# The last MLP of a two-layer graph kernel in three split passes, and the identity and two bias additions on GpSimd

## The chip, the cores and the metric

The kernel runs on one core of one Trainium2 chip. The metric is the device time of one execution in microseconds (us). Three executions of the kernel before gave 590.76, 591.12 and 591.52 us; the median is 591.12. In the profiled execution the granted TensorE clock was 0.998 of full speed (2.4 GHz).

## The reference, cut to what matters

`adj` is a 4096 x 4096 matrix A, `x` and `x2` are 4096 x 128. All is float32.

```
ax1 = A @ x ; ax2 = A @ x2
h1  = (2 + eps1) * ax1 ; h2 = (2 + eps2) * ax2
for i in range(3):                          # the MLP, for each of the two branches
    h1 = relu(h1 @ W1[i].T + b1[i]) ; h2 = relu(h2 @ W2[i].T + b2[i])
x   = layernorm(x + concat(h1, h2) @ Wm.T + bm)
Ah  = A + I ; d = rsqrt(rowsum(Ah))
out = layernorm(x + (d[:, None] * Ah * d[None, :]) @ x @ W.T + b)
```

## The kernel before, in words

**Split numbers.** A float32 matrix product is made from three passes of a faster format, fp32r: each operand is a rounded part `hi` and a rest `lo = value - hi`, and the passes are hi\*hi, hi\*lo and lo\*hi. For every tile of A (128 rows of 1024 columns, `raw`), ScalarE (ACT) rounds it to `ahi` (L723), VectorE (DVE) makes the rest `alo` (L920) and TensorE (PE) multiplies it (L536). `x1hi` and `x1lo` are the other operand, split the same way.

**Tiles and stages.** A layer is four quarters of 32 tiles. In layer 0 a tile takes 12 matmuls of 512 columns, for `x` and `x2`, and DVE also adds every tile to the row sums (L931, L935). In layer 1 it takes 6. Layer 1 is `ps <- (A + I) @ y`, where y is the normalised output of layer 0 times d. I stands on the diagonal, so it is added to one square of 128 x 128 in 32 of the 128 tiles, in place in `raw` (L1095 and L1102), before ACT rounds them. The tiles of layer 1 are called L1.0, L1.1 and so on here, in the order in which PE takes them. The first 24 are of quarter 0, then 8 of quarter 1, then the last 8 of quarter 0 (`woven`).

**Who runs ahead.** ACT rounds up to 4 tiles ahead of PE in layer 0 and 6 in layer 1 (the wait on `block_used` before L723), DVE follows ACT. Each engine runs a fixed list in program order; nothing is reordered when it runs.

**The MLP.** The MLP of a quarter runs in the quarter behind it, its steps slotted between tiles by tables: `PE_DENSE` (behind which tile PE runs each of the three dense layers), `PE_MERGE` (the product with Wm), `ACT_RELU`, `DVE_SPLIT_H`. The second entry of each pair, plan 1, is for the MLP of the last quarter, which runs beside the first tiles of layer 1. A dense step is four pieces `m` of 128 x 512. In plan 1 the first dense layer, behind tile L1.1, is plain float32 with `par` and `h` as they are; it waits for `h_ready` alone. The other two are split, in three passes with `hhi` (from ACT, L749) and `h_rest` (from DVE, L942).

**What hangs on the last MLP.** Merge, residual, statistics, the power of -0.5 on GpSimd (POOL, L1246), then `yt` and its rounding on ACT and `x1lo` on DVE (L1074), behind tile L1.25. PE needs them at L1.32. ACT then also writes the last quarter of `xn` (L756). The second residual bases (`xn <- xn + b`, L1079, 128 x 1024 each) are made on DVE, the third behind L1.58 and the fourth behind L1.92.

**GpSimd before.** It makes constants at the start and then only powers of 128 x 8 and smaller (L1241, L1246).

Of the kernel before, what the change touches and what calls it, by code (L numbers as in the profile page):

```python
# [37 lines left out]
M = 2 * CH  # L38
# [30 lines left out]
PE_DENSE = ({3: 0, 5: 1, 8: 2}, {1: 0, 3: 1, 5: 2})  # L69
PE_MERGE = (10, 6)  # L70
DVE_SPLIT_H = {4: 1, 6: 2}
# [6 lines left out]
ACT_RELU = ({k + SPLIT: l for k, l in PE_DENSE[0].items()}, {4: 0, 6: 1, 7: 2})  # L78
# [7 lines left out]
ACT_NORM_LAST = 29  # L86
# [4 lines left out]
ACT_NORM = (22, 20)  # L91
ACT_COPY_AY = 3
DVE_MAKE_Y = (KB + 4, 2 * KB + 4, 3 * KB + 3, 23)
# [3 lines left out]
DVE_SECOND_BASE = DVE_SPLIT_Y[:2] + (JB + 26, 2 * JB + 28)  # L97
AHEAD = 3
AHEAD2 = 5
# [23 lines left out]
def build(nc, a_t, head, early, x12, params, scratch, out):  # L123
    with ExitStack() as ctx:  # L124
# [368 lines left out]
        def _(pe):  # L493
# [48 lines left out]
            def dense(q, l, plan):  # L542

                for m in range(M):

                    if plan == 0:
                        wait(pe, hlo_ready, q * (LAYERS * M) + (M * l + m + 1))
                        passes = ((whi, hhi), (whi, hlo), (wlo, hhi))
                    elif l:
                        wait(pe, hlo_ready, q * (LAYERS * M) + (M * (l - 1) + m + 1))  # L550
                        passes = ((whi, hhi), (whi, h_rest), (wlo, hhi))
                    else:
                        wait(pe, h_ready, q * (4 * M) + (M * l + m + 1))
# [127 lines left out]
        def _(act):  # L681
# [214 lines left out]
        def _(dve):  # L896
# [40 lines left out]
            def split_h(q, l, m, plan):  # L937
# [3 lines left out]
                wait(dve, hhi_ready, q * (LAYERS * M) + (M * (l - plan) + m + 1))  # L941
# [148 lines left out]
            def add_identity(q, n):  # L1090

                wait_raw1(dve, q, n)
                k = n % KB
                square = raw_tile(1, n)[:, k * P:(k + 1) * P]
                dve.tensor_tensor(square, square, identity[:, :], ALU.add).then_inc(identity_added, 1)  # L1095

            def add_identities_last(n):

                wait_unit(dve, n)
                for at in squares_of(n):  # L1100
                    square = raw_tile(1, n)[:, at:at + P]
                    dve.tensor_tensor(square, square, identity[:, :], ALU.add).then_inc(identity_added, 1)  # L1102

# [28 lines left out]
            def layer0_quarter(q, before):  # L1132
                for n in range(JB):
# [8 lines left out]
                    if q is QUARTERS - 1:  # L1142
# [5 lines left out]
                        if n >= JB - KB:  # L1148
                            add_identity(0, n + KB - JB)

            def layer1_first():

                for p in range(2 * JB):
                    split_a(p // JB, 1, p % JB)
                    if p < JB:
                        mlp_step(LAST, p, 1)
                        y_step(p, (LAST,))
                        if p in DVE_SPLIT_H:
                            for m in range(M):
                                split_h(LAST, DVE_SPLIT_H[p], m, 1)  # L1160
                    finish_step(0, p - FIRST_ENDS - 1)
                    if p == DVE_SECOND_BASE[2]:
                        second_base(2)
                    if JB <= p and (p - JB + AHEAD2) // KB == 1:
                        add_identity(1, p - JB + AHEAD2)

            def layer1_quarter(q, before):
                for n in range(JB):
# [4 lines left out]
                    if q * JB + n == DVE_SECOND_BASE[3]:  # L1173
                        second_base(3)
                    if q == LAST:
                        for i in range(0 if n == 0 else n + AHEAD2, min(n + AHEAD2 + 1, JB)):
                            if squares_of(i):
                                add_identities_last(i)
                    elif (n + AHEAD2) // KB == q:
                        add_identity(q, n + AHEAD2)  # L1180
# [56 lines left out]
        def _(pool):  # L1237
# [4 lines left out]

            def norm_power(done, r=slice(0, KB)):
# [21 lines left out]
            for q in range(QUARTERS - 1):  # L1265
                norm_power(q + QUARTERS + 1)
# [45 lines left out]
```

## Time and profile before

| What | Value |
|---|---|
| median of 3 runs | 591.12 us |
| the profiled execution's own time | 591.38 us |
| its span, first to last instruction | 589.6 us |
| PE busy | 583.0 us, 99% |
| DVE busy | 545.4 us, 93% |
| ACT busy | 378.8 us, 64% |
| POOL busy | 28.1 us, 5% |

The span is the stretch from the first to the last instruction on the chip; the time holds 1.8 us more around it. Busy time of PE counts matmuls whose ends are modelled, so two starts in a row say more than a duration. On DVE and ACT a row's duration overlaps the next instruction a little: two DVE operations of 1024 columns last 1.21 us each and start 1.14 us apart. Where the text says pitch, it means from start to start.

### The profile page before, as it was taken

To read this page: it belongs to the slowest core of one execution; us is meant where nothing else is said; L and a number is where in the kernel's file an instruction comes from. 1 tells how busy PE (TensorE), PEld (TensorE's weight loads), DVE (VectorE), ACT (ScalarE), POOL (GpSimd) and SP (SyncE) were. 2 spreads that over 40 slices of the span, in tenths; PEclk is the share of its full clock that TensorE was granted. 3 is DMA by queue.
4 is the path that set the end of the run, shared out by engine and by line. 5 is a ranking of instruction groups with operands and counts; after the bars stand their busy time and mean duration, and the time that the engine had idled before them with its cause. 6 is when DMAs were issued, how large, how long until landed. Compare 5 with 4: busy or idle time off the path is not lost.

```text
span 589.6 us, 7659 instructions
## 1 busy us (share of the span) xinstructions
PE 583.0 (99%) x2676; PEld 485.9 (82%) x2676; DVE 545.4 (93%) x695; ACT 378.8 (64%) x512; POOL 28.1 (5%) x26
## 2 busy tenths in 40 slices
PE   9999999999999999999999999999999999999996
PEld 8888888888888888888888888878888888888885
DVE  6999999998988998898799999997999997989986
ACT  6544437852454773453667336479799799799794
POOL 0000000001100000110000020000200001010011
PEclk9999999999999999999999999999999999999999
DMA  8968565443655544354544374776899999999921
GB/s 330 397 248 294 206 223 206 145 148 143 207 196 179 179 169 145 142 197 178 195 147 143 143 268 187 261 287 222 316 365 392 425 377 340 387 338 367 387 77 72
DMA packets 31131, 141.91 MB, mean 241 GB/s; under 512 B 5504, under 2 KB 6272, under 8 KB 17024
## 3 DMA queue, kind: packets, MB, share of 16 engines
q1 hardware_dynamic: 30528, 139.87, 64.6%
q10 hardware_dynamic: 576, 1.70, 0.7%
q8 instruction: 14, 0.23, 0.2%
q14 instruction: 13, 0.11, 0.1%
HBM read 139.40 MB, written 2.16 MB: 240 GB/s over the span
## 4 chain that ended last, share of the span: by engine, by line
PE 97%; ACT 1%; DVE 1%; issue 1%; POOLq 0%; POOL 0%; DVEq 0%
PE ps L536 81%; PE pd L557 6%; PE ps L612 6%; PE pd L566 2%; PE pd L598 1%; PE pd L664 1%; ACT outn L756 0%; ACT ahi L723 0%; DVE z L1217 0%; ACT ahi_extra L723 0%; DVE stats L1222 0%; POOLq L124 0%; POOL rstd L1246 0%; DVE mv L1007 0%; DVE vareps L1014 0%
## 5 line engine op out<-in xcount | busy, mean ns | idle before, releaser
L723 ACT ACTIVATE ahi<-raw 128x1024 fp32r<-128x1024 f32 x212 | 222.6, 1060 | 162.5 <-PE ps L536 156.3
L920 DVE TENSOR_TENSOR alo<-raw,ahi 128x1024 fp32r<-128x1024 f32 x212 | 256.5, 1218 | 27.0 <-ACT ahi L723 26.0
L536 PE MATMUL ps<-ahi,x2s 128*128 128x512 f32 x512 | 138.4, 389 | 0.0
L536 PE MATMUL ps<-ahi,x1hi 128*128 128x512 f32 x384 | 121.9, 393 | 0.0
L536 PE MATMUL ps<-ahi,x1lo 128*128 128x512 f32 x384 | 120.9, 390 | 0.0
L536 PE MATMUL ps<-alo,x1hi 128*128 128x512 f32 x384 | 120.6, 390 | 0.0
L536 PEld LDWEIGHTS ps<-ahi,x2s 128*128 128x128 f32 x512 | 96.4, 188 | 20.1
L536 PEld LDWEIGHTS ps<-alo,x1hi 128*128 128x128 f32 x384 | 72.2, 188 | 15.1
L536 PEld LDWEIGHTS ps<-ahi,x1lo 128*128 128x128 f32 x384 | 72.3, 188 | 15.0
L536 PEld LDWEIGHTS ps<-ahi,x1hi 128*128 128x128 f32 x384 | 71.9, 188 | 15.0 <-issue 0.7
L536 PE MATMUL ps<-alo,x2s 128*128 128x512 f32 x256 | 80.2, 389 | 0.0
L931 DVE TENSOR_TENSOR rowsum<-rowsum,raw 128x1024 f32<-128x1024 f32 x60 | 73.0, 1216 | 0.0
L935 DVE TENSOR_TENSOR rowsum<-rowsum,raw 128x1024 f32<-128x1024 f32 x56 | 68.1, 1216 | 0.0
L536 PEld LDWEIGHTS ps<-alo,x2s 128*128 128x128 f32 x256 | 48.0, 188 | 10.0
L920 DVE TENSOR_TENSOR alo_extra<-raw,ahi_extra 128x1024 fp32r<-128x1024 f32 x42 | 50.8, 1221 | 3.9 <-ACT ahi_extra L723 3.6
L723 ACT ACTIVATE ahi_extra<-raw 128x1024 fp32r<-128x1024 f32 x42 | 43.8, 1060 | 2.7 <-PE ps L536 1.8
L744 ACT ACTIVATE h<-pd,par 128x512 f32<-128x512 f32 x48 | 31.8, 695 | 1.0 <-PE pd L557 1.0
L1246 POOL TENSOR_TENSOR rstd<-vareps,halves 128x8 f32<-128x8 f32 (+2 forms) x10 | 20.3, 2025 | 184.0 <-DVE vareps L1125 138.4
L1241 POOL TENSOR_TENSOR degpow<-degc,halves 128x8 f32<-128x8 f32 x4 | 6.6, 1640 | 373.6 <-DVE degpos L985 373.6
L942 DVE TENSOR_TENSOR hlo<-h,hhi 128x512 fp32r<-128x512 f32 x36 | 22.6, 683 | 0.0
L728 ACT ACTIVATE hhi<-h 128x512 fp32r<-128x512 f32 x36 | 22.0, 629 | 0.8
L536 PE MATMUL ps<-alo_extra,x1hi 128*128 128x512 f32 x64 | 20.0, 389 | 0.0
(103 smaller groups left out, 526.6 us busy)
## 6 DMA issues: line engine op xcount, KB each, us to landing
raw<-a_t SPq DMA_DIRECT2D x108, 1024.0 KB, 4.9
raw<-a_t SPq DMA_DIRECT2D x32, 512.0 KB, 7.4
raw<-early SPq DMA_DIRECT2D x7, 512.0 KB, 7.5
xn<-x SPq DMA_DIRECT2D x2, 1024.0 KB, 7.8
xn<-x SPq DMA_DIRECT2D x3, 512.0 KB, 10.5
out<-outn ACTq DMA_DIRECT2D x3, 512.0 KB, 6.6
par<-params SPq DMA_DIRECT2D x1, 708.0 KB, 12.4
raw<-head SPq DMA_DIRECT2D x2, 256.0 KB, 3.1
```

The lines of the kernel that those rows point to most:

```text
L536: mm = pe.matmul(ps[bank + (CH * (q % 2) if layer else 0)][:, :], block_of(w, n), a[c], start=(n == 0 and k == 0), stop=(n == JB - 1 and k ...
L557: mm = pe.matmul(pd[:, m, :], w[:, at:at + P], a[:, m, :], start=(k == 0), stop=(k == len(passes) - 1))
L566: mm = pe.matmul(merged[:, k, :], h[:, CH * b + k // 4, (k % 4) * P:(k % 4 + 1) * P], par[:, WM_AT + b * P:WM_AT + (b + 1) * P], start=(k ...
L612: mm = pe.matmul(bank, block_of(w, j + t), a[:, at], start=(n == opens and t == 0 and k == 0), stop=(n == closes and t == 1 and k == 2), s ...
L723: act.activation(ring_hi(layer, q, n), raw_tile(layer, n), ACT.Copy).then_inc(hi_ready, 1)
L728: act.activation(hhi[:, m, :], h[:, m, :], ACT.Copy).then_inc(hhi_ready, 1)
L744: act.activation(h[:, m, :], pd[:, m, :], ACT.Relu, bias=par[:, at:at + 1]).then_inc(h_ready, 1)
L920: dve.tensor_tensor(ring_lo(layer, q, n), raw_tile(layer, n), as_f32(ring_hi(layer, q, n)), ALU.subtract).then_inc(lo_ready, 1)
L931: dve.tensor_tensor(rowsum[:, :], rowsum[:, :], tile, ALU.add).then_inc(rowsum_step, 1)
L935: dve.tensor_tensor(to[:, :], rowsum[:, :], tile, ALU.add).then_inc(raw_used, 1)
L942: dve.tensor_tensor((hlo, h_rest)[plan][:, m, :], h[:, m, :], as_f32(hhi[:, m, :]), ALU.subtract).then_inc(hlo_ready, 1)
L1246: pool.tensor_tensor(rstd[:, r], vareps[:, r], halves[:, r], ALU.pow).then_inc(rstd_ready, 1)
```

## The change: what it does

1. The first dense layer of the last MLP becomes split, as the other two are: ACT rounds `h` to `hhi` (four pieces, behind its tiles 3 and 4), DVE makes `h_rest`, PE runs 12 passes in place of 4 plain float32 products. All three dense layers and the merge go behind later tiles: 4, 6, 8 and 10 in place of 1, 3, 5 and 6.
2. DVE makes `h_rest` in two parts, two pieces behind one tile and two behind the next, three times. Before it was four pieces behind one tile, twice.
3. The steps behind the merge go with it: `yt`, its rounding and `x1lo` come 4 tiles later (L1.29 for `x1lo`), and the last quarter of `xn` comes 3 tiles later.
4. The 32 additions of the identity and the second bases of quarters 2 and 3 go from DVE to GpSimd, in its program order: 8 identities, the powers of the last quarter, 8 identities, both bases, then powers and identities in turn.

```diff
-PE_DENSE = ({3: 0, 5: 1, 8: 2}, {1: 0, 3: 1, 5: 2})
-PE_MERGE = (10, 6)
-DVE_SPLIT_H = {4: 1, 6: 2}
+PE_DENSE = ({3: 0, 5: 1, 8: 2}, {4: 0, 6: 1, 8: 2})
+PE_MERGE = (10, 10)
+DVE_SPLIT_H = {3: (0, 0), 4: (0, 2), 5: (1, 0), 6: (1, 2), 8: (2, 0), 9: (2, 2)}
...
-ACT_RELU = ({k + SPLIT: l for k, l in PE_DENSE[0].items()}, {4: 0, 6: 1, 7: 2})
+ACT_RELU = ({k + SPLIT: l for k, l in PE_DENSE[0].items()}, {7: 0, 9: 1, 10: 2})
...
-ACT_NORM_LAST = 29
+ACT_NORM_LAST = 32
...
-ACT_NORM = (22, 20)
+ACT_NORM = (22, 24)
...
-DVE_MAKE_Y = (KB + 4, 2 * KB + 4, 3 * KB + 3, 23)
+DVE_MAKE_Y = (KB + 4, 2 * KB + 4, 3 * KB + 3, 27)
...
-                    elif l:
-                        wait(pe, hlo_ready, q * (LAYERS * M) + (M * (l - 1) + m + 1))
+                    else:
+                        wait(pe, hlo_ready, q * (LAYERS * M) + (M * l + m + 1))
                         passes = ((whi, hhi), (whi, h_rest), (wlo, hhi))
-                    else:
-                        wait(pe, h_ready, q * (4 * M) + (M * l + m + 1))
-                        passes = ((par, h),)
...
-                if plan == 0 and n in (ACT_EVACUATE[0] + 1, ACT_EVACUATE[0] + 2):
+                if n in (ACT_EVACUATE[plan] + 1, ACT_EVACUATE[plan] + 2):
                     for m in range(CH):
-                        round_h(q, 0, CH * (n - ACT_EVACUATE[0] - 1) + m)
+                        round_h(q, 0, CH * (n - ACT_EVACUATE[plan] - 1) + m)
...
-                        if n >= JB - KB:
-                            add_identity(0, n + KB - JB)
...
-                            for m in range(M):
-                                split_h(LAST, DVE_SPLIT_H[p], m, 1)
+                            l, first = DVE_SPLIT_H[p]
+                            for m in range(first, first + CH):
+                                split_h(LAST, l, m, 1)
...
+            for n in range(KB):
+                add_identity(0, n)
             degree_power(QUARTERS - 1)
             norm_power(QUARTERS)
...
+            for n in range(KB, 2 * KB):
+                add_identity(1, n)
+            pool.wait_ge(xn_ready, 2 * QUARTERS)
+            pool.wait_ge(yt_ready, LAST)
+            for q in range(2, QUARTERS):
+                pool.tensor_tensor(quarter(xn, q), quarter(xn, q), bias_rows(BO_AT), ALU.add).then_inc(base_ready, 1)
```

On DVE at the seam of the layers, the kernel before ran this. The first row is the identity of L1.7, the `x3` are the rests of L1.0 to L1.2, and the `alo` behind the reduction is that of L1.3:

```order
L1095 TENSOR_TENSOR raw<-raw,identity 128x128
L920 TENSOR_TENSOR alo<-raw,ahi 128x1024 x3
L964 STREAM_TRANSPOSE outn<-rowsum_all 128x1024
L970 TENSOR_REDUCE partial<-outn 128x32
L920 TENSOR_TENSOR alo<-raw,ahi 128x1024
L920 TENSOR_TENSOR alo_extra<-raw,ahi_extra 128x1024
L942 TENSOR_TENSOR h_rest<-h,hhi 128x512 x4
L920 TENSOR_TENSOR alo_extra<-raw,ahi_extra 128x1024
L920 TENSOR_TENSOR alo<-raw,ahi 128x1024
L942 TENSOR_TENSOR h_rest<-h,hhi 128x512 x4
```

The changed kernel runs this in the same place (its lines L915, L959, L965 and L937 are L920, L964, L970 and L942 of the kernel before):

```order
L915 TENSOR_TENSOR alo<-raw,ahi 128x1024 x3
L959 STREAM_TRANSPOSE outn<-rowsum_all 128x1024
L965 TENSOR_REDUCE partial<-outn 128x32
L915 TENSOR_TENSOR alo<-raw,ahi 128x1024
L937 TENSOR_TENSOR h_rest<-h,hhi 128x512 x2
L915 TENSOR_TENSOR alo_extra<-raw,ahi_extra 128x1024
L937 TENSOR_TENSOR h_rest<-h,hhi 128x512 x2
L915 TENSOR_TENSOR alo_extra<-raw,ahi_extra 128x1024
L937 TENSOR_TENSOR h_rest<-h,hhi 128x512 x2
L915 TENSOR_TENSOR alo<-raw,ahi 128x1024
L937 TENSOR_TENSOR h_rest<-h,hhi 128x512 x2
```

The identities are gone from DVE, and each of the rests of L1.4, L1.5, L1.6 and L1.7 now stands behind two pieces of `h_rest`.

On PE, the plain float32 layer stood behind the two first tiles of layer 1 (here the end of L1.0, then L1.1, the layer, and L1.2):

```order
L536 MATMUL ps<-alo,x1hi 128x512
L536 MATMUL ps<-ahi,x1hi 128x512 x2
L536 MATMUL ps<-ahi,x1lo 128x512 x2
L536 MATMUL ps<-alo,x1hi 128x512 x2
L557 MATMUL pd<-h,par 128x512 x4
L536 MATMUL ps<-ahi,x1hi 128x512 x2
L536 MATMUL ps<-ahi,x1lo 128x512 x2
L536 MATMUL ps<-alo,x1hi 128x512 x2
```

Now PE goes from tile L1.2 through L1.3 and L1.4 before it reaches the first piece of the split layer:

```order
L534 MATMUL ps<-ahi,x1hi 128x512 x2
L534 MATMUL ps<-ahi,x1lo 128x512 x2
L534 MATMUL ps<-alo,x1hi 128x512 x2
L534 MATMUL ps<-ahi,x1hi 128x512 x2
L534 MATMUL ps<-ahi,x1lo 128x512 x2
L534 MATMUL ps<-alo,x1hi 128x512 x2
L534 MATMUL ps<-ahi_extra,x1hi 128x512 x2
L534 MATMUL ps<-ahi_extra,x1lo 128x512 x2
L534 MATMUL ps<-alo_extra,x1hi 128x512 x2
L552 MATMUL pd<-hhi,whi 128x512
L552 MATMUL pd<-h_rest,whi 128x512
L552 MATMUL pd<-hhi,wlo 128x512
```

PE takes five tiles of A in a row there, where before it took two.

## Rows read from the trace of the kernel before

**Rows 1.** Part 1 of the page: engine, busy us, share of the span, instructions.
```profile
PE 583.0 (99%) x2676; PEld 485.9 (82%) x2676; DVE 545.4 (93%) x695; ACT 378.8 (64%) x512; POOL 28.1 (5%) x26
```

**Rows 2.** Waits of PE, whole span: us in total, times, longest.
```profile
PE pd L664 <- DVE blank L1182: 1.1, 1, 1.1
PE pd L598 <- DVE h L1211: 0.5, 1, 0.5
```

**Rows 3.** Timeline of PE at the seam of the layers: start us, us, what.
```profile
386.98 0.39 PE L536 MATMUL ps<-alo,x1hi 128*128 128x512 f32 x1
...
390.61 0.61 PE L536 MATMUL ps<-ahi,x1hi 128*128 128x512 f32 x2
...
391.51 0.62 PE L536 MATMUL ps<-alo,x1hi 128*128 128x512 f32 x2
391.97 3.59 PE L557 MATMUL pd<-h,par 128*128 128x512 f32 x8
...
396.77 0.62 PE L536 MATMUL ps<-ahi,x1hi 128*128 128x512 f32 x2
...
398.13 0.39 PE L557 MATMUL pd<-hhi,whi 128*128 128x512 f32 x1
...
400.85 0.62 PE L536 MATMUL ps<-ahi_extra,x1hi 128*128 128x512 f32 x2
```

**Rows 4.** Timeline of DVE before and at the seam, no idle time between.
```profile
368.16 0.27 DVE L1095 TENSOR_TENSOR raw<-raw,identity 128x128 f32<-128x128 f32 x1
368.36 1.21 DVE L920 TENSOR_TENSOR alo<-raw,ahi 128x1024 fp32r<-128x1024 f32 x1
...
385.47 1.21 DVE L920 TENSOR_TENSOR alo<-raw,ahi 128x1024 fp32r<-128x1024 f32 x1
...
387.95 3.48 DVE L920 TENSOR_TENSOR alo<-raw,ahi 128x1024 fp32r<-128x1024 f32 x3
391.35 1.23 DVE L964 STREAM_TRANSPOSE outn<-rowsum_all 128x1024 f32<-128x1024 f32 x1
...
393.75 1.22 DVE L920 TENSOR_TENSOR alo<-raw,ahi 128x1024 fp32r<-128x1024 f32 x1
...
396.01 2.54 DVE L942 TENSOR_TENSOR h_rest<-h,hhi 128x512 fp32r<-128x512 f32 x4
```

**Rows 5.** Timeline of ACT in its activations of the MLP.
```profile
393.61 0.68 ACT L749 ACTIVATE hhi<-pd,par 128x512 fp32r<-128x512 f32 x1
394.18 0.69 ACT L744 ACTIVATE h<-pd,par 128x512 f32<-128x512 f32 x1
```

**Rows 6.** Timeline of POOL: a one-input pass of 128 columns, then powers.
```profile
1.18 0.29 POOL L1250 TENSOR_SCALAR_AFFINE_SELECT identity<-identity 128x128 f32<-128x128 f32 x1 [0.24 <-POOL identity L1248]
...
240.83 1.64 POOL L1241 TENSOR_TENSOR degpow<-degc,halves 128x8 f32<-128x8 f32 x1 [84.62 <-DVE degpos L985]
252.43 2.57 POOL L1246 TENSOR_TENSOR rstd<-vareps,halves 128x8 f32<-128x8 f32 x1 [9.96 <-DVE vareps L1014]
```

**Rows 7.** Timeline of DVE around the second of those powers.
```profile
252.28 1.23 DVE L920 TENSOR_TENSOR alo<-raw,ahi 128x1024 fp32r<-128x1024 f32 x1
253.42 1.23 DVE L931 TENSOR_TENSOR rowsum<-rowsum,raw 128x1024 f32<-128x1024 f32 x1
254.57 1.21 DVE L920 TENSOR_TENSOR alo<-raw,ahi 128x1024 fp32r<-128x1024 f32 x1
255.70 1.21 DVE L935 TENSOR_TENSOR rowsum<-rowsum,raw 128x1024 f32<-128x1024 f32 x1
```

**Rows 8.** Timeline of DVE beside the first of those powers.
```profile
240.86 0.28 DVE L999 BATCH_NORM_STATS2 stats<-z 128x6 f32<-128x128 f32 x1
```

**Rows 9.** Timeline of DVE behind `x1lo`: rests of L1.26 and L1.27.
```profile
436.54 2.35 DVE L920 TENSOR_TENSOR alo<-raw,ahi 128x1024 fp32r<-128x1024 f32 x2
```

**Rows 10.** Timeline of PE: its first use of the rest of L1.26.
```profile
438.07 0.62 PE L536 MATMUL ps<-alo,x1hi 128*128 128x512 f32 x2
```

**Rows 11.** Timeline of ACT: the last block of `xn` of the last quarter.
```profile
447.25 0.49 ACT L756 ACTIVATE xn<-z,nshift,rstd 128x128 f32<-128x128 f32 x1
```

More of the change, by code:

```diff
@@ L96 @@
 DVE_SPLIT_Y = tuple(k + 2 for k in DVE_MAKE_Y)
-DVE_SECOND_BASE = DVE_SPLIT_Y[:2] + (JB + 26, 2 * JB + 28)
-AHEAD = 3
-AHEAD2 = 5
+DVE_SECOND_BASE = DVE_SPLIT_Y[:2]
 DVE_RESIDUAL2 = PE_PROJECT + SPLIT2
@@ L940, in split_h @@
                     wait(dve, h_ready, q * (4 * M) + (M * l + m + 1))
-                wait(dve, hhi_ready, q * (LAYERS * M) + (M * (l - plan) + m + 1))
+                wait(dve, hhi_ready, q * (LAYERS * M) + (M * l + m + 1))
                 dve.tensor_tensor((hlo, h_rest)[plan][:, m, :], h[:, m, :], as_f32(hhi[:, m, :]),
@@ L1088, in y_step @@
                         second_base(g)
[L1090 to L1102, printed above, removed]
             def residual2(q, k):
@@ L1158, in layer1_first @@
                         if p in DVE_SPLIT_H:
-                            for m in range(M):
-                                split_h(LAST, DVE_SPLIT_H[p], m, 1)
+                            l, first = DVE_SPLIT_H[p]
+                            for m in range(first, first + CH):
+                                split_h(LAST, l, m, 1)
                     finish_step(0, p - FIRST_ENDS - 1)
[L1162 to L1165, printed above, removed]
             def layer1_quarter(q, before):
@@ L1172, in layer1_quarter @@
                     finish_step(before, n)
[L1173 to L1180, printed above, removed]
             dve.memset(blank[:, :], 0.0).then_inc(blank_ready, 1)
@@ L1241, in degree_power, with add_identity, add_identities_last @@
                 pool.tensor_tensor(degpow[:, :], degc[:, :], halves[:, :], ALU.pow).then_inc(degpow_ready, 1)
+            def add_identity(q, n):
+                wait_raw1(pool, q, n)
+                k = n % KB
+                square = raw_tile(1, n)[:, k * P:(k + 1) * P]
+                pool.tensor_tensor(square, square, identity[:, :], ALU.add).then_inc(identity_added, 1)
+            def add_identities_last(n):
+                wait_unit(pool, n)
+                for at in squares_of(n):
+                    square = raw_tile(1, n)[:, at:at + P]
+                    pool.tensor_tensor(square, square, identity[:, :], ALU.add).then_inc(identity_added, 1)
             def norm_power(done, r=slice(0, KB)):
@@ L1262, in _ @@
                 norm_power(q + 1)
+            for n in range(KB):
+                add_identity(0, n)
             degree_power(QUARTERS - 1)
             norm_power(QUARTERS)
-            for q in range(QUARTERS - 1):
-                norm_power(q + QUARTERS + 1)
+            for n in range(KB, 2 * KB):
[4 more added lines that the diff above has]
+                pool.tensor_tensor(quarter(xn, q), quarter(xn, q), bias_rows(BO_AT), ALU.add).then_inc(base_ready, 1)
+            for q in range(2, QUARTERS):
+                if q == LAST:
+                    for n in range(JB):
+                        if squares_of(n):
+                            add_identities_last(n)
+                    norm_power(2 * QUARTERS - 1)
+                else:
+                    norm_power(QUARTERS + 1)
+                    for n in range(q * KB, q * KB + KB):
+                        add_identity(q, n)
+                    norm_power(QUARTERS + q)
             for g, (k0, k1) in enumerate(TAIL):
```

## The prediction

> **What bounds the kernel now.** I read part 1 of the page first: PE is busy 99% of the span, DVE 93% [rows 1]. Then the waits of PE: 1.1 us at the start and 0.5 us near the end, and none between [rows 2]. So the time is PE's own work, and only two things move it: less work on PE, or a wait that PE does not have now. The third view was the timeline of PE and DVE at the seam of the layers, to see how far DVE is ahead. The rest of the last tile of layer 0 is done at 385.47 + 1.21 = 386.68, and PE uses it at 386.98, 0.30 us later [rows 3, 4]. DVE runs without a gap there. So DVE is almost the bound at the seam.
>
> **PE's own work.** A tile of layer 1 takes 391.97 - 390.61 = 1.36 us. The plain float32 layer: it starts at 391.97, and L1.3 starts at 396.77, with L1.2 between, so it takes 396.77 - 1.36 - 391.97 = 3.44 us. A split layer takes 400.85 - 398.13 = 2.72 us [rows 3]. The gain is 3.44 - 2.72 = 0.72 us. The merge and all else of PE stay.
>
> **What DVE sheds.** An identity costs DVE 368.36 - 368.16 = 0.20 us of pitch [rows 4]. 8 of them stand ahead of L1.0 (7 ahead of the tile with 0.30 us left), 8 more beside L1.35 to L1.42, 16 later, where DVE has 2 us or more in hand for most tiles and PE waits for nothing: those are worth nothing. The second bases are shed late as well.
>
> **What it costs when POOL reads SBUF.** No row has a sum of this size on POOL. But the powers tell something. The same power of 128 x 8 lasts 1.64 us where POOL starts it beside a `BATCH_NORM_STATS2` of DVE, which has one input [rows 8], and 2.57 us where it starts 0.15 us into a rest of 1024 columns [rows 6, 7]. The surplus, 0.93 us, is what was left of that operation (253.42 - 252.43 = 0.99). So POOL waits for a DVE operation with two SBUF inputs. In the other direction the next DVE operation starts on time, at 253.42, inside the power, but it takes 254.57 - 253.42 = 1.15 us of pitch where its neighbour takes 1.13: some 0.01 to 0.015 us for the 8 columns that POOL reads. So the two share a read path, and DVE pays about the time that POOL reads. For 128 columns this is 16 times as much, 0.16 to 0.24 us; for 1024 columns 1.3 to 1.9. The bounds are 0 (no hold) and the 0.29 us of the one-input pass of 128 columns [rows 6], 8 times that or 2.3 us for a base. I take the value nearest to DVE's own pitch for the same columns, 0.2 us, and 1.6 for a base.
>
> The page SBUF — State Buffer of the Trainium skill (section Who interferes with whom) says that a VectorE instruction with two SBUF inputs contends with a GpSimd instruction that reads SBUF, and that whoever issues first has the pair for its whole instruction. By that rule, the trace agrees in one direction (POOL waited 0.93 us) and not in the other: DVE started at 253.42 inside a power that ran to 255.00. The GPSIMD Engine Reference (section 3.1) gives 4497 ns for a `tensor_tensor` add of 2048 float32 columns, so an estimate from that page is 2.25 us for one base and 0.28 for an identity.
>
> **Dense stage, step by step.** With 0.2 us an identity the 8 POOL additions (all done before L1.0: DVE finds the tiles landed for its own from 368.16 on [rows 4]) cost DVE what the 8 it sheds gave back. The rest of L1.0 starts at 387.95 as before, and the `alo` of L1.3 at 393.75, ready at 394.95 [rows 4]. PE has no dense layer ahead of it now: L1.3 starts at 390.61 + 2 x 1.36 = 393.33 and needs the rest 391.51 - 390.61 = 0.90 us later, at 394.23 [rows 3]. Wait: 0.7 to 0.8. Then DVE has 2 `h_rest` (2.54 / 4, or 0.62 of pitch each [rows 4]) ahead of the rest of L1.4: 394.89 + 1.24 + 1.21 = 397.34, while PE wants it at 394.23 + 0.75 + 1.36 = 396.34. Wait: 1.0. The dense layer then ends at 400.6. `relu` on ACT can start at 398.7, gives one `h` and one `hhi` every 1.14 us (2 x 0.57 [rows 5]), so the second `hhi` is there at 401.3. The rest of L1.6 is queued behind its `h_rest` on DVE: 401.3 + 0.62 + 1.21 = 403.1, and PE wants it at 400.6 + 1.36 + 0.90 = 402.85. Wait: 0.3. From L1.7 on PE's two dense layers give DVE 5.4 us and I find no further wait. Sum: 2.1 us. If POOL cost DVE nothing, DVE would be 1.6 us earlier, the first two waits would shrink to 0.2, and the sum would be 0.5 us: the last wait hangs on ACT and stays.
>
> **Behind the merge.** `x1lo` is 4 tiles later, and so is the low point of DVE's lead behind it: before, the rest of L1.26 is ready at 436.54 + 1.21 = 437.75 and used at 438.07, 0.3 us left [rows 9, 10]; now this is L1.30. From there DVE gains 1.36 - 1.14 = 0.22 us a tile, while the 8 identities that POOL adds there, as their tiles land, take 0.2 each. When POOL gets to the bases, DVE has about 0.5 us in hand and not the 2 it has before. They start when the last block of `xn` is done, which is at 447.25 + 0.49 now [rows 11] and 3 tiles and 2 us later after the change, near 454. Two bases of 1.6 us hold DVE 3.2 us, with one or two rests between; 3.2 - 0.5 - 2 x 0.2 = 2.3 us of wait, and 0.1 us at L1.30. The 1.7 us of the projection behind L1.41 come too late to help. Later identities on POOL cost DVE what it sheds.
>
> **Sum.** -0.72 + 2.1 + 0.1 + 2.3 = +3.8 us. The profiled execution took 591.38 us (span 589.6), which makes 595.2; it lies 0.26 us over the median of 591.12, so on the scale of the median I forecast 594.9 us. What a measurement of this kernel can tell from no change is 0.2%, 1.2 us.
>
> **The rivals.**
>
> *No hold: DVE really is relieved.* Then POOL's sums are free, DVE is 1.6 us earlier at the seam and PE waits 0.5 us in the dense stage: -0.72 + 0.5 = -0.2 us, 590.9. For it: DVE starts on time inside a power. Against it: the 0.93 us that POOL loses, and the 0.01 us of DVE behind the power. It decides where an identity costs DVE under 0.07 us, for then the two first waits of the dense stage stay under 0.5 us and the gain of PE covers them. It cannot be faster by more than 0.72 us, 0.12%, since no other work of PE goes. This is the side on which the forecast of slower is wrong.
>
> *Identities hold DVE, the bases do not.* A long sum on POOL could be read in pieces between DVE's operations, or come when DVE has more in hand than my 0.5 us. Then the last term falls away: -0.72 + 2.1 = +1.4, or 592.5. For it: POOL always gave way to an operation under way. Against it: even in pieces the columns are the same.
>
> *POOL holds for its whole operation.* With 0.29 us an identity and 2.3 a base: the last tile of layer 0 waits 8 x 0.29 - 7 x 0.20 - 0.30 = 0.6 us, the dense stage 2.2, behind L1.30 it loses 0.3 and some 0.06 a tile, and the bases 2 x 2.3 - 0.7: together 0.6 + 2.2 + 0.6 + 3.9 - 0.7 = +6.6, 597.7. It is the rule of the page above with a price from a row; DVE's start at 253.42 speaks against it.
>
> **How the numbers follow.** I give the forecast 0.45, the bases without a hold 0.18, no hold at all 0.25, the hold of the whole operation 0.12. Range: from the rival without a hold (590.8) to just below the whole hold (597.4). Slower by over 0.2%: 0.45 + 0.12 + most of 0.18 makes 0.72. Within 0.2%: 0.25, which is the rival without a hold and a part of the second. Faster by over 0.2% needs more than PE has to give: 0.03.
>
> **What would show it.** In the profile after: the first dense layer as 12 passes in 2.72 us; waits of PE on `alo` at L1.3, L1.4 and L1.6 of 0.7, 1.0 and 0.3 us and again of 1 us and more near 456 and 458 us, beside the two bases on POOL; POOL's identities lasting 1 us and more where they start inside a DVE operation, and DVE operations of 1.4 us instead of 1.2 beside them. If the rests of DVE keep a pitch of 1.14 us beside POOL's sums, the hold is wrong, and with it 1.6 us of the dense stage and all of the last term. If waits of PE stand at the bases and not at the seam, the chain of the dense stage is wrong.

## The result and the profile after

The changed kernel takes 599.16 us (median of 4 executions, 598.23 to 600.42) against 591.32 us of the kernel before, measured beside it (4 executions). The ratio is 1.0131 with a 95% interval of 1.0117 to 1.0145: it is slower by 7.8 us. The forecast was slower by 3.8 us, to 594.9, and its range ended at 597.4. The sign held; the size did not.

The profiled execution took 598.23 us with a span of 596.4; before it was 591.38 and 589.6. Part 1 of the page after answers to [rows 1]:

```profile
PE 585.3 (98%) x2680; PEld 486.6 (82%) x2680; DVE 548.9 (92%) x665; ACT 381.0 (64%) x516; POOL 82.6 (14%) x60
```

DVE has 30 instructions less and is busy 3.5 us more. The waits of PE, of which before only those for `blank` and `h` stood there [rows 2]:

```profile
PE ps L534 <- DVE alo L915: 3.8, 2, 2.1
PE pd L659 <- DVE blank L1150: 1.1, 1, 1.1
PE ps L534 <- DVE alo_extra L915: 0.7, 1, 0.7
PE pd L593 <- DVE h L1179: 0.5, 1, 0.5
```

The view lists no wait below some tenths, so the timeline of PE is read by starts. A pair of matmuls takes 0.45 us from start to start. At the seam of the layers, in place of [rows 3]:

```profile
393.63 0.61 PE L534 MATMUL ps<-ahi,x1lo 128*128 128x512 f32 x2
394.32 0.73 PE L534 MATMUL ps<-alo,x1hi 128*128 128x512 f32 x2
...
395.35 0.62 PE L534 MATMUL ps<-ahi_extra,x1lo 128*128 128x512 f32 x2
396.66 0.72 PE L534 MATMUL ps<-alo_extra,x1hi 128*128 128x512 f32 x2 [0.69 <-DVE alo_extra L915]
397.22 0.40 PE L552 MATMUL pd<-hhi,whi 128*128 128x512 f32 x1
...
399.98 0.61 PE L534 MATMUL ps<-ahi_extra,x1hi 128*128 128x512 f32 x2
...
401.79 0.61 PE L534 MATMUL ps<-ahi,x1lo 128*128 128x512 f32 x2
402.52 0.72 PE L534 MATMUL ps<-alo,x1hi 128*128 128x512 f32 x2
```

The rest of L1.3 comes 394.32 - 393.63 - 0.45 = 0.24 us late, that of L1.4 0.86 and that of L1.6 0.28; each time the matmuls behind the wait start another 0.11 late. The split layer takes 399.98 - 397.22 = 2.76 us. The second place is beside the two bases on POOL:

```profile
455.22 0.63 PE L534 MATMUL ps<-ahi,x1lo 128*128 128x512 f32 x2
457.53 0.74 PE L534 MATMUL ps<-alo,x1hi 128*128 128x512 f32 x2 [1.69 <-DVE alo L915]
...
458.35 0.40 PE L534 MATMUL ps<-ahi,x1lo 128*128 128x512 f32 x1
460.84 0.79 PE L534 MATMUL ps<-alo,x1hi 128*128 128x512 f32 x1 [2.10 <-DVE alo L915]
461.43 0.63 PE L534 MATMUL ps<-ahi,x1hi 128*128 128x512 f32 x1
461.86 0.63 PE L534 MATMUL ps<-ahi,x1lo 128*128 128x512 f32 x1
...
463.56 0.86 PE L534 MATMUL ps<-ahi_extra,x1lo 128*128 128x512 f32 x2
```

PE waits 1.86 + 0.11 and 2.27 + 0.36 us. Then six matmuls start 0.43 us apart in place of 0.227. The table by stretches of the same kernel gives the granted clock. Behind the length of the stretch stand the busy us of PE, of its weight loads, of DVE, ACT and POOL, each with its instructions; the last three columns are the granted clock of PE, the DMA share and GB/s:

```profile
456.00:460.00 4.00, 1.21 (x4) 0.67 (x4) 4.00 (x2) 0.86 (x1) 3.70 (x2) 1.00 0.59 242
460.00:462.00 2.00, 1.16 (x3) 0.97 (x4) 2.00 (x3) 0.33 (x1) 0.00 (x0) 0.66 0.21 25
462.00:465.00 3.00, 3.00 (x11) 2.34 (x10) 3.00 (x3) 2.32 (x4) 0.00 (x0) 0.66 0.90 333
```

PE was busy 1.21 of the 4 us between 456 and 460; behind that its clock was at the lower level, 1.2 GHz, for a part of two stretches, then back at 2.4. That costs 6 x 0.20 us, and 0.25 of the 0.36 above.

What POOL does, in place of [rows 6], and the VectorE operations beside it:

```profile
353.49 2.53 POOL L1216 TENSOR_TENSOR raw<-raw,identity 128x128 f32<-128x128 f32 x2
...
376.19 14.85 POOL L1216 TENSOR_TENSOR raw<-raw,identity 128x128 f32<-128x128 f32 x1 [17.21 <-DMA raw<-a_t]
...
453.15 6.55 POOL L1254 TENSOR_TENSOR xn<-xn,par 128x1024 f32<-128x1024 f32 x2
```

```profile
354.22 1.48 DVE L1064 TENSOR_TENSOR yt<-xn,dall 128x1024 f32<-128x1024 f32 x1
355.62 1.48 DVE L915 TENSOR_TENSOR alo<-raw,ahi 128x1024 fp32r<-128x1024 f32 x1
...
387.24 3.48 DVE L915 TENSOR_TENSOR alo<-raw,ahi 128x1024 fp32r<-128x1024 f32 x3
390.64 1.23 DVE L959 STREAM_TRANSPOSE outn<-rowsum_all 128x1024 f32<-128x1024 f32 x1
...
454.06 6.72 DVE L915 TENSOR_TENSOR alo<-raw,ahi 128x1024 fp32r<-128x1024 f32 x2
```

An operation of DVE beside an identity lasts 1.48 us and not 1.21: an identity holds DVE 0.27 us. The two rests beside the bases take 460.71 - 454.06 = 6.65 us from start to start (the next row of that view starts at 460.71); without a hold it would be 2 x 1.135 = 2.27. So a base holds DVE 2.19 us. And one identity took 14.85 us: it started at 376.19 and ended at 391.04, in the transpose.

### The profile page after: what moved, and what is told of

It is laid out like the page before. It is cut to its first block, busy times and chain, and to the rows that moved or that the text cites. A ratio compares the mean times of both kernels' runs of the same rounds, so it can differ in the third digit from the quotient of the medians.

```text
span 596.4 us, 7680 instructions
## 1 busy us (share of the span) xinstructions
PE 585.3 (98%) x2680; PEld 486.6 (82%) x2680; DVE 548.9 (92%) x665; ACT 381.0 (64%) x516; POOL 82.6 (14%) x60
## 4 chain that ended last, share of the span: by engine, by line
PE 81%; DVE 9%; ACT 6%; issue 2%; POOL 1%; POOLq 0%; DVEq 0%; ACTq 0%
PE ps L534 72%; DVE alo L915 5%; PE pd L552 4%; DVE alo_extra L915 2%; PE pd L561 2%; ACT ahi L718 2%; ACT h L739 1%; POOL rstd L1228 1%; PE pd L593 1%; ACT hhi L744 1%; ACT ahi_extra L718 1%; PE ps L607 1%; PE pd L659 1%; ACT outn L808 1%; ACT yt L781 0%
## 5 line engine op out<-in xcount | busy, mean ns | idle before, releaser
L915 DVE TENSOR_TENSOR alo<-raw,ahi 128x1024 fp32r<-128x1024 f32 x212 | 263.0, 1249 | 25.6 <-ACT ahi L718 23.7
L915 DVE TENSOR_TENSOR alo_extra<-raw,ahi_extra 128x1024 fp32r<-128x1024 f32 x42 | 51.6, 1239 | 7.8 <-ACT ahi_extra L718 7.1
L1216 POOL TENSOR_TENSOR raw<-raw,identity 128x128 f32<-128x128 f32 x24 | 37.8, 1597 | 42.8 <-DMA raw<-a_t 42.8
L723 ACT ACTIVATE hhi<-h 128x512 fp32r<-128x512 f32 x40 | 24.4, 630 | 0.8
L937 DVE TENSOR_TENSOR hlo<-h,hhi 128x512 fp32r<-128x512 f32 x36 | 22.6, 681 | 0.0
```

The source lines that it names most:

```text
L723: act.activation(hhi[:, m, :], h[:, m, :], ACT.Copy).then_inc(hhi_ready, 1)
L915: dve.tensor_tensor(ring_lo(layer, q, n), raw_tile(layer, n), as_f32(ring_hi(layer, q, n)), ALU.subtract).then_inc(lo_ready, 1)
L937: dve.tensor_tensor((hlo, h_rest)[plan][:, m, :], h[:, m, :], as_f32(hhi[:, m, :]), ALU.subtract).then_inc(hlo_ready, 1)
L1216: pool.tensor_tensor(square, square, identity[:, :], ALU.add).then_inc(identity_added, 1)
```

## The experiments

The kernel before was run beside each group: 591.71 us for the first four (14 executions), 591.50 for the next four (19), 591.79 for the d group and c2 (13), 591.51 for c3 and c4 (21). Intervals are of the ratio to it. "Theory 1" is that of the prediction with the sizes read from the trace after.

| Kernel | us | ratio, 95% | against before |
|---|---|---|---|
| a1 the split last MLP alone | 593.77 | 1.0036, 1.0022 to 1.0050 | +2.1 |
| a2 the POOL additions alone | 595.37 | 1.0073, 1.0051 to 1.0095 | +3.7 |
| a3 changed, bases on DVE | 593.21 | 1.0025, 1.0015 to 1.0034 | +1.5 |
| a4 changed, identities on DVE | 598.10 | 1.0108, 1.0091 to 1.0125 | +6.4 |
| a5 = a1 with 8 narrow identities | 593.17 | 1.0023, 1.0013 to 1.0034 | +1.7 |
| b1 changed, bases 40 us later | 595.47 | 1.0064, 1.0048 to 1.0079 | +4.0 |
| b2 changed, bases in 16 pieces | 595.84 | 1.0073, 1.0058 to 1.0089 | +4.3 |
| c1 = a1 in another order | 592.26 | 1.0009, 1.0000 to 1.0018 | +0.8 |
| c2 = c1, fourth base behind L1.108 | 593.62 | 1.0028, 1.0018 to 1.0038 | +1.8 |
| c3 = c1, both bases into gaps of DVE | 591.75 | 1.0007, 0.9998 to 1.0017 | +0.2 |
| c4 = before, bases moved as in c3 | 591.72 | 1.0001, 0.9992 to 1.0010 | +0.2 |
| d0 changed kernel again, one execution | 597.56 | | |
| d1 changed, one base on POOL | 595.69 | 1.0070, 1.0056 to 1.0084 | +3.9 |
| d2 changed, 8 small operations more | 601.07 | 1.0168, 1.0147 to 1.0190 | +9.3 |

### The two parts apart

a1 has parts 1 to 3 of the change and leaves the additions on DVE; a2 has part 4 alone.

> Only the MLP part of the change; the identities and all four second bases stay on VectorE. Theory 1 (what GpSimd reads holds VectorE back, and the MLP's new order costs only the waits of the dense stage): PE gains 0.72 us and waits 0.8 + 1.0 + 0.3 = 2.1 us at L1.3, L1.4 and L1.6, so +1.4 us against the kernel before (some 592.7), and no wait of PE near 456 us, no stretch at half clock. Rival (the MLP's new order is the cause, GpSimd innocent): +5 us or more, with the two long waits near 456 us still there.

> Only the GpSimd part of the change; the MLP as in the kernel before. Theory 1: no wait at the seam (four identities at 0.27 us take less from VectorE than eight at 0.20 gave back), but the two bases on GpSimd hold VectorE 2.2 us each with some 1.3 us in hand, so PE waits about 3 us near 455 us, and perhaps 1 us more at half clock: +3 to +4 us (594.5). Rival (the MLP is the cause): within 1 us of the kernel before.

The waits of PE in a1, then in a2 (without the two that every kernel has):

```profile
PE ps L536 <- DVE alo_extra L917: 0.7, 1, 0.7
PE ps L536 <- DVE alo L917: 0.6, 1, 0.6
...
PE ps L609 <- DVE alo L917: 0.3, 1, 0.3
```

```profile
PE ps L536 <- DVE alo_extra L920: 3.0, 3, 1.7
```

So each part is slower by itself, and by its own waits: the first at the seam, the second beside the bases. a2 has nothing at the seam. Its two waits beside the bases come to 3.03 us by starts; the third of the view stands far behind them, at 538.8 us, and costs 0.79. By starts the seam of a1 costs 2.24 us, which with the 0.7 gained makes 1.5; the other 0.6 us of its 2.1 are taken up with c1. Neither shows a lower clock there. 2.1 + 3.7 = 5.8, and the change costs 7.8; by the spans of the profiled executions it is 2.2 + 3.9 = 6.1 against 6.8. In the change the bases find DVE without a lead and the clock falls; against that, its profile lacks the waits near 536 to 539 us that a1 and a2 have, and its seam costs 0.5 us less than that of a1.

### Which addition costs

```diff
+                    if q * JB + n == DVE_SECOND_BASE[3]:      # a3: bases back on DVE (third likewise)
+                        second_base(3)
```

> The whole change, but the last two second bases back on VectorE where they were. Theory 1: the waits of 1.9 and 2.3 us and the 1.2 us at half clock near 456 to 464 us go, the dense stage keeps its 1.7 us: +1.0 to +1.5 us against the kernel before (592.5). Rival (identities on GpSimd are the heavier part): +4 us or more.

> The whole change, but the 32 identities back on VectorE; the last two second bases on GpSimd. Theory 1: dense stage 2.1 us, bases 4.4 us of hold with 1.0 us in hand and 0.4 us gained between, so 3 us of wait, then 0 to 1.2 us at half clock: +4.5 to +5.5 us (596.3). Rival (identities are the heavier part): under +2 us.

With the identities alone on POOL (a3) the time is that of a1 within the intervals. The profile of a3 has 0.5 us less of wait at the seam (0.35 us in place of 0.90 at L1.3), and that is what moving the identities off DVE gave there. a4 cost 6.4 us, a little over theory 1, but by another path. Its first base did not hold DVE where it was issued; it was shut out itself. POOL in a4:

```profile
454.22 17.41 POOL L1262 TENSOR_TENSOR xn<-xn,par 128x1024 f32<-128x1024 f32 x2 [22.12 <-ACT xn L753]
```

The first of the two lasted 14.07 us and got in only when DVE came to its first `z <- pd` operation, at 465.95. That operation was not held; the rest behind it was, for 1.94 us, and likewise with the second base. So both holds fell on the chain from `z` to the normalised output, and PE waited for its end at the projection:

```profile
498.16 2.05 PE L595 MATMUL pd<-par,h 128*128 128x128 f32 x16 [2.19 <-ACT h L802]
```

### Is the price the reading time, and is it paid anywhere

b1 has POOL add the bases behind its next power, near 493 us. b2 adds them at the old place in 16 pieces of 128 columns.

```diff
+                for k in range(KB):                           # b2
+                    i = pool.tensor_tensor(quarter(xn, q)[:, k:k + 1, :], quarter(xn, q)[:, k:k + 1, :], ...)
```

> The whole change, with the two bases on GpSimd moved behind the power of the first quarter of layer 1 (near 494 us), where VectorE is 5 us or more ahead. Theory 1 (a base on GpSimd holds VectorE some 2.2 us, and it costs time only where VectorE is not ahead): VectorE's operations beside the bases still take 3.4 us, but PE does not wait for them and stays at full clock; the time is that of the kernel with the bases on VectorE, +1.5 us against the kernel before (593.2). Rival (the place matters little; GpSimd's two long additions cost some 5 us wherever they stand): +6 us or more.

> The whole change, with each of the two bases on GpSimd written as 8 additions of 128 columns. Theory 1 (the hold is GpSimd's reading time, 0.27 us for 128 columns, taken once for each of its instructions): the same 4.3 us of hold, but one piece beside each VectorE operation, so VectorE makes up 0.22 us a tile in between: no wait over 0.6 us, no half clock, +2.0 to +3.0 us against the kernel before. Rival (the hold is mostly a fixed price of each GpSimd instruction, over 0.3 us): 16 instructions cost 8 us or more of hold and the time is no better than the change's own, +7 us.

The bases of b2, then the first of b1, then what DVE did beside that one:

```profile
454.04 22.32 POOL L1271 TENSOR_TENSOR xn<-xn,par 128x128 f32<-128x128 f32 x16
```

```profile
492.98 2.39 POOL L1271 TENSOR_TENSOR xn<-xn,par 128x1024 f32<-128x1024 f32 x1
```

```profile
493.05 2.35 DVE L1127 TENSOR_TENSOR nshift<-nmean,rstd 128x8 f32<-128x8 f32 x1 [0.40 <-POOL rstd L1244]
```

An operation of 8 columns, which takes 0.17 us in the kernel before, took 2.35: the hold, 2.2 us, does not depend on what DVE does. In b2 the 16 pieces follow each other every 1.40 us. Ten of them hold a rest of DVE 0.27 us each. From 468.93 us on DVE alternates between `z <- pd` and rests; the last six pieces get in beside the `z` and hold nothing. The last two held rests and the first free one:

```profile
466.13 2.88 DVE L917 TENSOR_TENSOR alo_extra<-raw,ahi_extra 128x1024 fp32r<-128x1024 f32 x2
...
469.20 1.22 DVE L917 TENSOR_TENSOR alo<-raw,ahi 128x1024 fp32r<-128x1024 f32 x1
```

So the hold in b2 is 10 x 0.27 = 2.7 us in all and not the 4.3 that theory 1 had. A fixed price of each GpSimd instruction is refuted even so: 8 pieces of 0.27 make the 2.19 of one base. In pieces or later, the long waits and the lower clock go (the largest wait beside the bases of b2 is 0.37 us), and the time falls from 599.2 to 595.8 and 595.5. Theory 1 had said +2 to +3 for b2 and +1.5 for b1. It missed what comes later: PE waits 1.1 us at the projection for `h` from ACT, and 0.4 to 0.5 near 539 us for `ahi`. By the order of the instructions the pause of DVE is handed on through the chain `nmean`, squares, `vareps`, power, `nshift`, output; no run cuts this chain.

### The seam

a5 is a1 with the first 8 identities added in one column of 128 only, so part of the identity is left out. That takes about 1 us off DVE ahead of L1.0.

```diff
+                width = 1 if q == 0 else P
+                dve.tensor_tensor(square[:, 0:width], square[:, 0:width], identity[:, 0:width], ALU.add)
```

> Only the MLP part, all additions on VectorE, and the first eight identities are added in one column of their squares instead of 128 (this leaves out part of the computation): VectorE is relieved of about 0.13 us each, 1.0 us before L1.0. Theory 1 (the waits at L1.3 and L1.4 hang on how far VectorE is behind at the seam, the one at L1.6 on ScalarE): PE waits 1.1 us instead of 2.1 in the dense stage, +0.4 us against the kernel before, 1 us under the kernel with the MLP part alone. Rival (the waits hang on the order alone): no less than that kernel, +2 us.

The waits at the seam fell by 1.0 us, from 2.24 to 1.23, so DVE's lateness is what PE waits for there. The time fell by 0.4 only; in this profile 0.5 us of wait also stands near 112 us, in layer 0, where nothing was edited. c1 takes nothing off DVE and changes its order: the rests of L1.3, L1.4 and L1.6 come ahead of the `h_rest`, the reduction of the row sums moves from behind L1.2 to behind L1.5, and the last dense layer comes one tile later.

```diff
+PE_DENSE = ({3: 0, 5: 1, 8: 2}, {4: 0, 6: 1, 9: 2})
+DVE_SPLIT_H = {4: 0, 6: 1, 9: 2}
+DVE_REDUCE_LAST = 5
+ACT_RELU = (..., {7: 0, 9: 1, 11: 2})
```

> The MLP part with everything on VectorE, and VectorE's order changed: the reduction of the transposed row sums (1.14 us) moves from behind L1.2 to behind L1.5, the four h_rest of the first dense layer stand behind the rest of L1.4 and those of the second behind L1.6, those of the third behind L1.9; the third dense layer runs behind L1.9 and its relu behind ScalarE's tile 11. Theory 1 (the dense stage loses only because h_rest and the reduction stand ahead of the rests of L1.3, L1.4 and L1.6): PE waits 0.2 us in all, and 0.5 us of the 0.72 us of PE's gain is left: -0.5 us against the kernel before (0.999). Rival (VectorE is short of time there, whatever the order): waits of 1 us or more come back elsewhere and it is +0.5 us or slower.

No matmul between 385 and 417 us is late in c1. From the first matmul behind the merge of the third quarter to the first behind the projection of layer 1's first quarter, the kernel before takes 460.63 - 332.03 = 128.60 us and c1 461.62 - 333.63 = 127.99. So PE's gain of 0.6 us is there. To the first matmul behind a later projection it is 564.41 - 332.03 = 232.38 and 566.19 - 333.63 = 232.56: all of it is lost again. (This profile is of the slowest of 11 executions and has 1.4 us of wait in layer 0, so only differences inside layer 1 are taken from it.) The waits of PE in c1 that the kernel before does not have (the first is in layer 0):

```profile
PE pd L555 <- DVE hlo L940: 0.6, 1, 0.6
...
PE ps L610 <- DVE alo L918: 0.3, 1, 0.3
PE ps L537 <- DVE alo L918: 0.2, 1, 0.2
```

### Where the gain of the shorter layer goes

The last two stand near 536 and 539 us, just behind the fourth base, and a1, a3 and a5 have one or both. Three kernels asked why. c2 moves that base far back; c3 moves both bases to where DVE waits for ACT anyway; c4 is c3's control.

```diff
-DVE_SECOND_BASE = DVE_SPLIT_Y[:2] + (JB + 26, 2 * JB + 28)
+DVE_SECOND_BASE = DVE_SPLIT_Y[:2] + (JB + 26, 3 * JB + 12)      # c2
+DVE_SECOND_BASE = DVE_SPLIT_Y[:2] + (2 * JB + 3, 2 * JB + 27)   # c3, c4
```

> The reordered split layer (all additions on VectorE) with the fourth second base behind tile L1.108 in place of L1.92. In the reordered kernel PE waited 0.38 us near 536 and 0.32 us near 539, just behind that base and four identities, where VectorE is the later engine by 1 us against the kernel before, since it has four pieces of h_rest (2.5 us) more. Theory 1 (those waits are what is left of its +0.5 us): they go, nothing comes in their place, and the time is 0.7 us under the reordered kernel's: 0.2 us under the kernel before, 591.3 if that has 591.5, ratio 0.9997. Theory 2 (the rest of the +0.5 us is in the start of the kernel and has nothing to do with the edit): no wait at 536 to 542, and the ratio stays 1.0009.

> The reordered split layer with both last second bases moved, all additions on VectorE: the third from behind L1.58 to behind L1.67, the fourth from behind L1.92 to behind L1.91. Both new places are just ahead of a stretch in which VectorE waits for ScalarE anyway (1.73 us at 494.4 us and 0.82 us at 529.9 in the reordered kernel). Theory 1 (what the reordered kernel loses is that VectorE, with 2.5 us of h_rest more, is 1 us later against TensorE, so that the chain nmean, squares, vareps, nshift, normalisation, ahi is late at 536 to 540 us): the chain is 1.1 us earlier, PE waits nowhere between 385 and 565 us, and the time is 0.6 to 0.7 us under the reordered kernel's 592.3 and under the kernel before by 0.3: 591.4 where that has 591.7, ratio 0.9995. Theory 2 (the place of the bases has nothing to do with it, as the base moved to L1.108 seemed to say): the waits of 0.36 and 0.29 us near 535 and 538 stay, ratio 1.001 to 1.002.

> The kernel before with the same two bases moved to the same places and nothing else. Theory 1: PE waits nowhere in that stretch already, so nothing is won: ratio 1.000 within 0.001. Theory 2 (moving the bases is worth something or costs something by itself): ratio outside of 0.999 to 1.001.

In c2 the waits stayed, now mostly for `ahi` from ACT, and a new one of 0.8 us came at a projection, at 565.5 us, for `h` from ACT. Both of its theories fell: the waits stayed, and moving the base cost. c3 is where the kernel before is, within the interval, and no better: theory 2 was right on the waits, and the ratio lies between the two. c4 is as forecast. Its waits:

```profile
PE ps L610 <- DVE alo L918: 0.3, 1, 0.3
PE ps L537 <- ACT ahi L698: 0.2, 1, 0.2
```

They are still there. The reason is in DVE's first rest behind the normalisation of the first output quarter, in c3 and then in c4:

```profile
492.68 1.23 DVE L918 TENSOR_TENSOR alo<-raw,ahi 128x1024 fp32r<-128x1024 f32 x1 [0.59 <-ACT ahi L721]
```

```profile
492.78 1.23 DVE L920 TENSOR_TENSOR alo<-raw,ahi 128x1024 fp32r<-128x1024 f32 x1 [0.59 <-ACT ahi L723]
```

The base was absorbed in both (the idle time before this rest is 0.59 us and not the 1.73 of c1), but the rest itself starts at the same time, though PE is 1.05 us earlier in c3 (first projection of the next quarter at 494.37 against 495.42). What sets it starts at `nmean`, at 474.66 us in c3 and 474.42 in the kernel before, and the bases stand behind that. I read this as DVE and ACT setting the pace of the chain from about 440 to 540 us; this is argued from the timelines, and no run tests it by itself. In the kernel before, DVE has 0.4 us in hand there, at its least. PE's 0.7 us come on top, DVE is 0.2 to 0.4 us later for its four `h_rest` more, and PE waits for the difference. So the shorter layer on PE is worth nothing that shows in any of these orders. That this would turn if DVE had less to do between 440 and 474 us was not tried.

### The clock and the shut-out

> The changed kernel once more, for one profile. In its first profile TensorE's granted clock was 0.66 in the two stretches 460 to 462 and 462 to 465 us, and six matmuls there started 0.43 us apart in place of 0.227, which cost 1.2 us. Theory 1: the fall of the clock belongs to this order of waits (1.86 and 2.27 us, 3 us apart, beside the two bases on GpSimd) and comes again; span 596.4 us within 0.3. Theory 2: it was a chance of that one execution; the waits are the same, the clock stays near 1, and the span is 595.2 us.

> The changed kernel with only the third second base on GpSimd; the fourth goes back to VectorE behind tile L1.92, where the kernel before has it. Theory 1 (each base on GpSimd holds VectorE 2.2 us, and two long waits in a row bring the clock down): the wait near 455 us stays at 1.9 us, the one near 458 (2.3 us) goes, the six slow matmuls (1.2 us) go, and up to 0.3 us comes back behind L1.92; 599.2 - 2.4 - 1.2 + 0.3 = 595.9 us. Theory 2 (the clock falls after any wait of near 2 us): the slow stretch stays, 597.1 us. Theory 3 (the cost is in the late chain, not in the hold): under 1 us is won, 598.2 or more.

> The changed kernel with one small VectorE operation more behind each of the last 8 tiles of layer 0 (a copy of 128 x 8, one SBUF input, near 0.08 us). In the changed kernel one identity on GpSimd began at 376.19 us and ended at 391.04, just after VectorE's first operation with one input (the transpose at 390.64). Theory 1 (between back-to-back VectorE operations with two SBUF inputs GpSimd does not get in, and any operation with one input lets it in): no identity on GpSimd lasts over 2.7 us, all 8 are made before 389 us and hold VectorE 0.27 us each, so the rest of L1.0 comes 4 x 0.27 + 8 x 0.08 = 1.7 us later and the waits of the dense stage grow by about as much: 600.5 to 601 us. Theory 2 (the small operation lets nothing in, or what let GpSimd in at 391 was something else): one identity again lasts over 10 us, only the 0.6 us of the small operations are added: 599.8 us.

d0 is the changed kernel unchanged. In this execution the transfers let POOL come to the bases at 455.7 us and not 453.15. The same table by stretches, of d0 and then of d1 and d2:

```profile
456.00:460.00 4.00, 2.95 (x13) 1.87 (x11) 4.00 (x2) 3.77 (x6) 4.00 (x2) 1.00 0.98 340
462.00:465.00 3.00, 1.49 (x11) 1.40 (x12) 3.00 (x3) 0.75 (x2) 0.38 (x1) 1.00 0.53 131
```

```profile
456.00:460.00 4.00, 2.31 (x10) 1.43 (x9) 4.00 (x3) 1.66 (x3) 0.82 (x1) 1.00 0.71 277
```

```profile
460.00:462.00 2.00, 0.06 (x1) 0.06 (x1) 2.00 (x2) 0.00 (x0) 0.80 (x1) 0.88 0.00 0
462.00:465.00 3.00, 3.00 (x7) 2.40 (x8) 3.00 (x3) 1.55 (x3) 0.00 (x0) 0.51 0.59 180
```

In d0 PE waits 1.39 and 1.84 us (0.11 more behind each), the clock stays at 1.00 and the time is 597.56 us. It has another wait that the first profile has not, 0.75 us at 541.0 for `alo_extra`. In d1 the wait of 1.86 us stands alone, the clock stays at 1.00 and the time is 595.69, as theory 1 had it (595.9): the second base and what follows it are worth 3.5 us. In d2 the waits are 1.86 and 2.27 again, and the slow stretch is there again. So the two profiles with both of these waits have the fall. Those with 1.39 and 1.84 us (d0), with 0.97 and 1.84 (a2), with 1.86 alone (d1) or with over 2 us alone (a4, at 498 us) have not. More than that the runs do not show.

Of the changed kernel's five executions two were profiled. Their mean granted clock was 0.995 with the slow stretch and 0.999 without it; the other three had 0.993 (599.34 us), 0.999 (598.98) and 0.996 (600.42). The one with 0.999 very likely had no slow stretch and is still 1.4 us above d0, and no profile shows what it lost.

d2 has one small operation with one SBUF input behind each of the last 8 tiles of layer 0.

```diff
+                        if n >= JB - KB:
+                            dve.tensor_scalar(spare[:, n + KB - JB, :], halves[:, :], 1.0, None, ALU.mult)
```

POOL and DVE in d2:

```profile
375.77 3.90 POOL L1219 TENSOR_TENSOR raw<-raw,identity 128x128 f32<-128x128 f32 x2 [17.39 <-DMA raw<-a_t]
380.48 5.57 POOL L1219 TENSOR_TENSOR raw<-raw,identity 128x128 f32<-128x128 f32 x2 [0.81 <-DMA raw<-a_t]
```

```profile
375.50 1.21 DVE L1065 TENSOR_TENSOR yt<-xn,dall 128x1024 f32<-128x1024 f32 x1
376.64 0.44 DVE L1131 TENSOR_SCALAR spare<-halves 128x8 f32<-128x8 f32 x1
376.99 1.21 DVE L916 TENSOR_TENSOR alo<-raw,ahi 128x1024 fp32r<-128x1024 f32 x1
...
379.26 0.44 DVE L1131 TENSOR_SCALAR spare<-halves 128x8 f32<-128x8 f32 x1
```

No identity lasts 14 us any more; the longest is 2.95 (theory 1 had said 2.7 at most). Four of the small operations last 0.43 or 0.44 us, which is the 0.16 of the other four and the hold of 0.27, and the operations with two inputs between them keep 1.21. So the small operation is what lets POOL in. The price came as expected too: PE now waits 1.03 + 0.11 us for the last rest of layer 0, which it uses at 387.25, and 0.5 us more at L1.3, together the 1.7 of theory 1. The times say less than the profile: they are 599.24 (the profiled one), 599.94, 602.20 and 602.78 us, and the median of 601.07, near the 600.5 to 601 of theory 1, lies between two pairs.

## Why the prediction was wrong

The sum, term by term, against the profiled execution:

| Term | forecast | measured |
|---|---|---|
| PE's own work | -0.72 | 3.44 - 2.76: -0.68 |
| waits at L1.3, L1.4, L1.6 | 0.75 + 1.0 + 0.3 | 0.35 + 0.97 + 0.39 |
| wait at L1.30 | 0.1 | 0.11 |
| waits beside the bases | 2.3 | 1.97 + 2.38 = 4.35 |
| lower clock behind them | none | 0.25 + 1.20 = 1.45 |
| sum | +3.8 | +6.9 |

The span grew by 6.8 us. The median grew by 7.8; the profiled execution is the fastest of four, and where the others lose another 0.7 to 2.2 us no profile shows. A wait near 540 us like that of d0 (0.75 us) may be a part of it.

**The mechanism of the hold was right.** PE waits at the three tiles and beside the two bases that the prediction named, POOL waits for a two-input operation of DVE, and DVE pays POOL's reading time. "No hold" is refuted, by every DVE operation of 1.48 us, and so is "identities hold, the bases do not". The hold for the whole operation is refuted for short ones: an identity that has nothing in its way lasts 0.47 us and DVE loses 0.27, a power lasts 1.64 and DVE loses 0.01 or so. For a base it is nearly right: the 3.25 us on POOL hold a wait of 0.9, one that gets in at once lasts 2.39 (b1), and DVE loses 2.19. That rival got 0.12, but its prices of 0.29 and 2.3 us were the nearest, and so was its sum of +6.6, 597.7 us.

**The step that failed is the term of the bases, +2.3 us, where 4.35 of wait and 1.45 of lower clock were measured.** Three things are in it: the size of the hold, the lead of DVE and the clock. The prediction scaled the 0.01 to 0.015 us that DVE lost beside a power of 8 columns to 128 and 1024 columns, and took DVE's own pitch, 0.2 and 1.6 us. Measured are 0.27 and 2.19. A loss of 0.01 us, read from rows rounded to 0.01, cannot be scaled by 16 and 128; the upper bounds that were worked out beside it, 0.29 and 2.3, were nearly right. The estimate from the GPSIMD Engine Reference (section 3.1) of the Trainium skill was 0.28 and 2.25 us: this trace agrees with it for the hold on DVE, while the additions themselves last 0.2 us longer on POOL, 0.47 and 2.39 us, where nothing is in their way. For two bases the difference is 1.2 us. The rest of the wait was the lead: 0.9 us were counted in hand, and there was none. With 0.27 an identity, those that POOL adds from 442 to 453 us take more than DVE gains there. Two holds make 2 x 2.19 = 4.38 us, and PE waited 4.35.

**The clock was missed.** 1.45 us of the error of 3.1 in the sum are PE at its lower level behind two waits that leave it idle 4.1 of 5.4 us. No term spoke of what a long wait does to PE itself. The clock alone does not explain the miss: d0 had no slow stretch and took 597.56 us, still just over the range.

**The seam was 0.35 us better than forecast.** Only four of the eight identities held DVE ahead of L1.0. One was shut out from 376 to 391 us and the other three behind it ran beside the transpose and the reduction, which cost DVE nothing. DVE shed 8 x 0.20 = 1.6 and paid 4 x 0.27 = 1.1, so it starts L1.0 at 387.24 us and not 387.95 (0.15 of this is an earlier start of the whole kernel). The waits at L1.4 and L1.6 came within 0.1 us.

**The rival on the other side had little to win.** Its best case was -0.72 us. c1 and c3 show that with all waits at the seam gone the shorter layer still brings nothing: PE waits for DVE and ACT near 536 to 539 us instead.

## What to carry to other kernels

An addition moved from VectorE to GpSimd is not taken off VectorE: here it cost VectorE 0.27 us where it had cost 0.20, and 2.19 where it had cost 1.14. It cost VectorE nothing beside the transpose, the reduction and `z <- pd`. Look at whose deadline the pause falls on: later or in pieces the bases still cost 2.3 to 2.6 us more on GpSimd than on VectorE (b1 and b2 against a3). Before shortening the busiest engine, find the least lead of the engine that feeds it: here it was 0.4 us, and nothing of the 0.7 was won. And a forecast of two waits of about 2 us close together on TensorE needs a second term for its clock.

## What the runs showed of the hardware

GpSimd can be shut out for long. With VectorE in back-to-back operations of two SBUF inputs, an addition on GpSimd that takes 0.47 us by itself lasted 14.85 us, 14.73 in d0 and 14.68 in a2, and a base in a4 that takes 2.39 by itself lasted 14.07. It ended at an operation of another kind: the transpose, `z <- pd`, or the small copy of d2. But two inputs do not always shut it out: the base at 453.15 us and the powers of the kernel before got in between two such operations [rows 6, 7]. What tells the two cases apart stays open.

Where it is in, the hold falls on the next operation of VectorE that it touches, and its length depends on GpSimd's columns and not on VectorE's: a base holds a two-input operation of 1024 columns and one of 8 for 2.2 us. The one-input copy of 8 columns in d2 is held as well, 0.27 us by an identity. The transpose, the reduction and `z <- pd` are not held. What decides this beyond these kinds was not tested.
